# Three graph layers and an edge-gated layer on one core: the end of a layer woven into its last turns

## The reference

```python
for i in range(3):
    msg = h[src]
    agg = segment_sum(msg, dst);  cnt = segment_sum(ones, dst)
    h = (agg / clip(cnt, 1)[:, None]) @ Wl[i] + bl[i] + h @ Wr[i]
    if i < 2: h = relu(h)
x = layernorm(x + h)
```

## Time and profile before

| what | value |
|---|---|
| three runs, us | 3498.85, 3500.41, 3501.01 (median 3500.41) |
| profiled execution, us | 3502.18, span 3500.4 |
| busy share of the span | PE 76%, POOL 67%, DVE 61%, ACT 35% |
| gathers of the three layers on POOL | 1584, 1538.5 us busy |
| mean granted TensorE clock | 0.905 of full speed |

### The profile page before, as it was taken

One profiled execution on the slowest core, in us unless ns is written; L12 is line 12 of the kernel. 1 busy time (PEld: TensorE's weight loads), 2 busy tenths in 40 slices (PEclk: granted clock), 3 DMA queues, 4 the chain that ended last, 5 costly groups with the idle time before them and its releaser, 6 DMA issues.

```text
span 3500.4 us, 71571 instructions
## 1 busy us (share of the span) xinstructions
PE 2665.2 (76%) x16221; PEld 2000.1 (57%) x16222; DVE 2142.4 (61%) x4932; ACT 1216.7 (35%) x1668; POOL 2333.4 (67%) x2399
## 2 busy tenths in 40 slices
PE   6578988656787775567887855678888888888884
PEld 5345555556564555555555555556666666666653
DVE  6644554446532234467454454668888888888886
ACT  2422333002000000020000000368888888888865
POOL 3567777575777777746777777357777777767610
PEclk8799999777899997788999977899999999999987
DMA  4354444223565562236887642254444444444411
GB/s 149 104 180 147 145 129 145 76 50 108 160 168 146 139 161 60 53 104 205 250 240 222 192 122 58 78 154 126 128 126 127 127 126 127 124 114 121 114 52 37
DMA packets 345986, 454.45 MB, mean 130 GB/s; under 512 B 135643, under 2 KB 260599, under 8 KB 342311
## 3 DMA queue, kind: packets, MB, share of 16 engines
q0 software_dynamic: 88624, 207.58, 21.9%
q10 hardware_dynamic: 101984, 181.27, 16.2%
q1 hardware_dynamic: 155304, 64.77, 7.1%
HBM read 357.03 MB, written 101.90 MB: 131 GB/s over the span
## 4 chain that ended last, share of the span: by engine, by line
POOL 35%; PE 21%; issue 19%; DVE 10%; DMA 9%; DVEq 3%; SPq 2%; ACT 2%; POOLq 0%; ACTq 0%
POOL shared L760 28%; POOL shared L800 8%; DMA shared<-q_dram,idx 6%; PE ps L955 6%; PE ps L946 4%; PE ps L1151 3%; PE ps L938 2%; SPq L638 1%; DVE work L2326 1%; PE ps L965 1%; DVE work L2010 1%; PE ps L1154 1%; DMA counts_dram<-work 1%; DVE work L2335 1%; ACT work L1481 1%
## 5 line engine op out<-in xcount | busy, mean ns | idle before, releaser
L760 POOL DMA_INDIRECT shared<-y_dram,idx x1584 | 1538.5, 971 | 623.3 <-issue 498.9
L946 PE MATMUL ps<-shared,work 128*128 x4368 | 683.0, 306 | 389.9 <-SPq L578 190.6
L800 POOL DMA_INDIRECT shared<-q_dram,idx x784 | 777.6, 992 | 284.0 <-issue 204.9
L946 PEld LDWEIGHTS ps<-shared,work 128*128 128x128 f32 x4368 | 618.6, 216 | 466.7 <-issue 457.1
L2037 DVE TENSOR_TENSOR acc<-acc,ps 128x129 f32 x546 | 156.3, 286 | 901.8 <-PE ps L946 770.9
L1151 PE MATMUL ps<-pq,work 128*128 x1664 | 498.8, 402 | 149.9 <-issue 89.6
L2326 DVE TENSOR_TENSOR work<-ps,shared 128x256 f32<-128x256 f32 x832 | 294.6, 416 | 177.6 <-PE ps L1154 149.4
L1151 PEld LDWEIGHTS ps<-pq,work 128*128 128x128 f32 x1664 | 257.5, 195 | 244.3 <-issue 173.6
L965 PE MATMUL ps<-pq,work 128*128 128x385 bf16 x1456 | 294.1, 352 | 73.2 <-DVE pq L2007 31.3
L1452 ACT ACTIVATE pq<-ps,blT_sb 128x512 f32<-128x512 f32 (+1 forms) x28 | 16.5, 631 | 887.6 <-PE ps L1050 887.6
L1333 ACT CAST work<-ps 128x600 bf16<-128x600 f32 x260 | 159.6, 661 | 339.6 <-PE ps L938 312.5
(11 more groups left out here) (363 smaller groups left out, 3627.2 us busy)
## 6 DMA issues: line engine op xcount, KB each, us to landing
work<-counts_dram ACTq DMA_DIRECT2D x156, 384.0 KB
counts_dram<-work ACTq DMA_DIRECT2D x26, 1568.0 KB
shared<-y_dram,idx POOLq DMA_INDIRECT x1584
ea_parts<-work ACTq DMA_DIRECT2D x128, 196.0 KB
ea_sb<-ea_parts SPq DMA_DIRECT2D x196, 128.0 KB
work<-counts_dram ACTq DMA_DIRECT2D x52, 416.0 KB
shared<-q_dram,idx POOLq DMA_INDIRECT x784
y_dram<-work SPq DMA_DIRECT2D x21, 448.0 KB, 3.0
```

What stands on the lines that cost most here:

```text
L760: pool.indirect_dma_start(msg[:, u, 0:F], None, y_dram, bass.IndirectOffsetOnAxis(ap=idx[:, u:u + 1], axis=0)).then_inc(s_quad[q], 16)
L800: pool.indirect_dma_start(q_ring[:, u * 2 * F:(u + 1) * 2 * F], None, q_dram, bass.IndirectOffsetOnAxis(ap=idx[:, u:u + 1], axis=0)).then_ ...
L946: last = te.matmul(ps[:, SUM_BANKS[i], 0:FA], lhsT=oh4[:, OH_SLOTS[i], u, :], rhs=shared[:, bass.ds(place + u * FA, FA)], start=u == 0, st ...
```

## The change

The end of layers 1 and 2 is moved into the last turns of pairs. `dst` is sorted, so low windows are complete before high ones: from turn `TAIL` = 3 on, turn 3 + c works on chunk c, for c from 0 to 5. Chunk 6 is done after the last turn. Within such a turn DVE computes the new rows after item 0 and clears that seventh of `acc` after item 1, PE transposes after item 2, multiplies with Wl after item 4 and with Wr after item 6, all through one place in PSUM (`ps_tail`, banks 6 and 7); ACT does the relu, all copies and the store of y. Since gathers still read this layer's y then, the next layer's y goes to another home in DRAM: `y_two[0]` for layers 1 and 3, `y_two[1]` for layer 2. New rows and staged y lie in `shared`, over parts of the split that are used up.

In layers 1 and 2 the one-hots of the pair turns take `iota`, as `ps_tail` shares bank 7 with `iota_ps`. `conv_rows` moves into layer 1, after POOL's first 48 gathers, with a wait on `y_split`; the copy to `dst_sorted` moves ahead of the first index loads on SP; the columns are made in the first pair turn of layer 1. The loops over pair turns of these layers are written out.

```diff
-        y_dram = dram("y_dram", (NP, F))
+        y_two = [dram("y_even", (NP, F)), dram("y_odd", (NP, F))]
...
+        h_two = [shared[:, Y_AT + k * CW * F:Y_AT + (k + 1) * CW * F].rearrange("p (u f) -> p u f", f=F) for k in range(2)]
+        y_next = [shared[:, Y_AT + k * CW * F:Y_AT + (k + 1) * CW * F].rearrange("p (u f) -> p u f", f=F) for k in range(2, 4)]
...
+        ps_tail = ps_flat[:, 6 * 512:6 * 512 + CW * F].rearrange("p (u f) -> p u f", f=F)
...
+        TAIL = DTURNS - NCH + 1
...
@@ sync
+            with sp.If(unsorted < 1):
+                sp.dma_start(dst_sorted, dst[0:EP].rearrange("(t e) -> t e", e=P)).then_inc(s["idx_given"], 16)
             sp.wait_ge(s["chosen"], 9)
...
                 first_indices()
-                for it in range(NCH):
-                    sp.wait_ge(s["prod_act"], ((layer + 1) * NCH + it + 1) * 2 + 1)
-                    sp.wait_ge(s["prod_dve"], ((layer + 1) * NCH + it + 1) * 2 + 1)
-                    sp.dma_start(y_dram[it * CW * P:(it + 1) * CW * P, :].rearrange("(u p) f -> p u f", p=P),
-                                 y_staged(it % 2)).then_inc(s[Y_SENT[it % 2]], 16)
...
@@ gpsimd
             def conv_rows():
                 pool.wait_ge(s["idx_given"], 16)
                 pool.wait_ge(s["tki"], 1)
+                pool.wait_ge(s["y_split"], NCH)
...
-                            msg[:, u, 0:F], None, y_dram,
+                            msg[:, u, 0:F], None, y_two[layer % 2],
...
                     for q in range(FIRST_SLOTS, RQ):
                         gathers(0, q)
+                    conv_rows()
...
             sage_gathers(0)
-            conv_rows()
@@ tensor
-                with pe.Fori(0, DTURNS) as b:
+                def both(b, after=None):
                     places = load_turn(b + WOVEN)
                     pairs = load_pairs(b)
                     for i in range(IT):
                         item(b + WOVEN, i, places[i])
                         pair_item(b, i, pairs[i])
+                        if after is not None:
+                            after(i)
...
+                def chunk_after(it):
+                    def after(i):
+                        if i == 2:
+                            transposes(layer, it)
+                        if i == 4:
+                            y_products(layer, it, ps_tail)
+                        if i == 6:
+                            res_products(layer, it, ps_tail)
+                    return after
...
+                    for b in range(TAIL):
+                        both(b, columns_after if layer == 0 and b == 0 else None)
+                    for b in range(TAIL, DTURNS):
+                        both(b, chunk_after(b - TAIL))
+                    transposes(layer, NCH - 1)
+                    y_products(layer, NCH - 1, ps_first(0))
+                    res_products(layer, NCH - 1, ps_first(1))
...
+            def transposes(layer, it):
+                c = layer * NCH + it
+                pe.wait_ge(s["dlo_ready"], 1)
+                if c:
+                    pe.wait_ge(s["res_kept"], c * 2)
+                for k, wins in enumerate(QUADS):
+                    pe.wait_ge(s["h_ready"], c * CW + wins[-1] + 1)
+                    for u in wins:
+                        last = te.transpose(ps_tail[:, u, :], h_two[it % 2][:, u, :], ident[:, :])
+                    last.then_inc(s["h_transposed"], 1)
...
@@ scalar
-                relu(0)
                 for it in range(NCH):
                     c = layer * NCH + it
+                    y_ps, res_ps = (ps_tail, ps_tail) if it < NCH - 1 else (ps_first(0), ps_first(1))
                     for k, wins in enumerate(QUADS):
                         act.wait_ge(s["h_transposed"], c * 2 + k + 1 + 1)
-                        sc.activation(h_all[...], ps_tr[...], ACT.Relu, ...)
+                        sc.activation(h_all[...], ps_tail[...], ACT.Relu, ...)
+                    if it >= 2:
+                        act.wait_ge(s[Y_SENT[it % 2]], y_sent(layer, it - 2))
+                    for k, wins in enumerate(QUADS):
+                        act.wait_ge(s["products"], c * 2 + k + 1)
+                        sc.copy(y_next[it % 2][:, wins[0]:wins[-1] + 1, :], y_ps[:, wins[0]:wins[-1] + 1, :]).then_inc(s["prod_act"], 1)
+                    act.wait_ge(s["prod_act"], (NCH + c) * 2 + 3)
+                    alone(act)
+                    act.dma_start(y_two[(layer + 1) % 2][it * CW * P:(it + 1) * CW * P, :].rearrange("(u p) f -> p u f", p=P),
+                                  y_next[it % 2]).then_inc(s[Y_SENT[it % 2]], 16)
+                    for k, wins in enumerate(QUADS):
+                        act.wait_ge(s["res_ready"], c * 2 + k + 1)
+                        sc.copy(chunk(res, it, F)[...], res_ps[...]).then_inc(s["res_kept"], 1)
@@ vector
-                onehots(layer, it * IT + (i + OHS - 1), columns[i], OH_SLOTS[(i + OHS - 1) % IT])
+                onehots(layer and not beside_tail, it * IT + (i + OHS - 1), columns[i], OH_SLOTS[(i + OHS - 1) % IT])
...
-                       in0=(iota_ps if layer else iota[:, :])           # pair_onehots
+                       in0=(iota_ps if layer == 2 else iota[:, :])
...
                         add_pair(layer, b, i, p_sums, p_columns)
+                        if conv and i == 5:
+                            conv_columns_known()
+                        if ending is not None and i == 0:
+                            dve.wait_ge(s["counts_put"], pair_added(layer, b, i))
+                            new_h(layer, ending)
+                        if ending is not None and i == 1:
+                            clear(layer, ending)
...
+                    for b in range(TAIL, DTURNS):
+                        both(b, ending=b - TAIL)
+                    dve.wait_ge(s["added_items"], (layer + 1) * NI1 + OHS)
+                    dve.wait_ge(s["counts_put"], pairs_added(layer + 1))
+                    new_h(layer, NCH - 1)
+                    clear(layer, NCH - 1)
...
+            def new_h(layer, it):
+                c = layer * NCH + it
+                if not layer:
+                    inverse_counts(it)
+                if c >= 2:
+                    dve.wait_ge(s["h_transposed"], c * 2 - 1)
+                for u in range(CW):
+                    w = it * CW + u
+                    v.scalar_tensor_tensor(
+                        out=h_two[it % 2][:, u, :], in0=acc[:, w * FA:w * FA + F], scalar=inv[:, w:w + 1],
+                        in1=res[:, w * F:(w + 1) * F], op0=ALU.mult, op1=ALU.add).then_inc(s["h_ready"], 1)
+
+            def clear(layer, it):
+                dve.wait_ge(s["h_ready"], layer * NW + (it + 1) * CW)
+                v.memset(acc[:, it * (CW * FA):(it + 1) * (CW * FA)], 0.0).then_inc(s["acc_clear"], 1)
...
-                v.memset(acc[:, :], 0.0).then_inc(s["acc_clear"], NCH)
```

More of the change, by code:

```diff
@@ L915, in sage_sums @@
                 pe.wait_ge(s["prod_act"], (layer + 1) * (NCH * 2) + 1)
[L916 removed]
+                pe.wait_ge(s["prod_dve"], NCH * 2 + 1)
                 if layer:
@@ new lines, in sage_sums @@
+                if layer == 2:
+                    pe.wait_ge(s["dlo_ready"], 1)
+                    with pe.Fori(0, DTURNS) as b:
+                        both(b)
+                else:
+                    for b in range(TAIL):
[5 more added lines that the diff above has]
+                    res_products(layer, NCH - 1, ps_first(1))
@@ new lines, in y_products, with res_products @@
+            def y_products(layer, it, to):
+                c = layer * NCH + it
+                for k, wins in enumerate(QUADS):
+                    pe.wait_ge(s["h_copied"], c * 2 + k + 1 + 1)
+                    for u in wins:
+                        last = te.matmul(to[:, u, :], lhsT=h_all[:, it * CW + u, :], rhs=w0_sb[:, layer + 1, 0:F], start=True, stop=True)
+                    last.then_inc(s["products"], 1)
+            def res_products(layer, it, to):
+                c = layer * NCH + it
+                for k, wins in enumerate(QUADS):
+                    if it < NCH - 1:
+                        pe.wait_ge(s["prod_act"], (NCH + c) * 2 + k + 1 + 1)
+                    for u in wins:
+                        last = te.matmul(to[:, u, :], lhsT=h_all[:, it * CW + u, :], rhs=w0_sb[:, layer + 1, F:2 * F], start=True, stop=True)
+                    last.then_inc(s["res_ready"], 1)
@@ L1085, in _ @@
+            for layer in range(3):
+                sage_sums(layer)
             pe.wait_ge(s["added_items"], 3 * NI1 + OHS)
@@ L1453, in relu @@
                                       ACT.Relu, bias=blT_sb[:, layer:layer + 1]).then_inc(s["h_copied"], 1)
-                relu(0)
-                for it in range(NCH):
-                    c = layer * NCH + it
-                    if it + 1 < NCH:
-                        relu(it + 1)
-                    act.wait_ge(s["y_free"], c + NCH)
-                    act.wait_ge(s["products"], c * 2 + 1)
```

(24 more changed lines are left out.)

132 lines of the change are left out of this document (35 added, 97 removed).

## The result

The changed kernel takes 3456.18 us (median of four, 3452.32 to 3456.57), the kernel before 3499.63 on the same chip: ratio 0.9872, interval 0.9860 to 0.9884. The profiled execution took 3456.49 with a span of 3454.7, so the two traces differ by 45.7.

What follows compares the result with a forecast made beforehand. POOL's gathers and its stops were taken as the bound; -31.1 (layer ends) - 13.5 (layer starts) + 11 (one-hots) + 8.8 (new rows) = -24.8, from the median 3500.4 to 3475 us, range 3465 to 3492.

Steps and rivals of the forecast that it cites:

- What bounds: Layers 1 to 3: a layer lasts as long as its 528 gathers, changing only if gathers lengthen or POOL stands still.
- End of layers: Ends of layers 1 and 2: only the seventh chunk is left, so first gathers come 15.0 and 16.1 us earlier.
- (e): Layer ends: seventh chunk lacks an empty pipe because chunk 5 is late; gain under 28 us; included in likeliest case's 0.50.
- Start of layers 2 and 3: Index-load stops some 65 us into each layer shrink because the split of y begins earlier: 13.5 us gained.
- One-hots of layer 2: Layer 2's pair turns: one-hots reading iota from SBUF instead of PSUM hold POOL's gathers, costing 11 us.
- Rival (b): Layer 2's one-hots cost what layer 1's dense stretch shows, 21.8 us instead of 11: 3486; chance 0.14.
- (d): POOL is held through most two-input DVE work beside gathers: at 90%, 90 us against 44.6 gained, 3546; chance 0.07.
- New rows beside the gathers: Six chunks in each of layers 1 and 2: seven-instruction DVE runs of 1.92 us hold gathers, costing 8.8 us.
- Rival (a): New rows cost POOL almost nothing, as it is released after each instruction: 3.5 us or under, 3470; chance 0.18.
- In layer 1 nothing changes here: Layer 1's pair turns already take one-hots from iota, so their cost to gathers stays the same: no term.
- Small things: Moved row conversion, dst copy, extra DVE and PE work and stores on ACT's queue: hidden or idle, priced at nothing.
- (c): PE becomes the bound in the tail turns, losing 2 us more in each of 12: 3499, no change; chance 0.11.

Runs made afterwards that it cites:

- the late read: Changed kernel, with ACT waiting for the first landed quad of layers 2 and 3 before reading y back for the split: 3467.38 us, ratio 0.9902.
- Runs of 14 and 21: Changed kernel, new-rows instructions of a chunk done twice (14 unbroken): 3484.81 us; three times (21): 3510.04 us, or 3491.61 with the real rows first.
- early rows: Kernel before, with POOL's seven row gathers after its first 48 gathers and the dst copy ahead of the first index loads: 3498.74 us, ratio 0.9999.
- a pause: One 0.4 us DVE clearing ahead of layer 1's pair turns: 3500.03 us in the kernel before, 3457.59 us in the changed kernel.
- two homes: Kernel before, with y in two homes in DRAM and nothing else: 3498.85 us against 3500.69, ratio 0.9994.
- three runs of seven: Changed kernel, new rows done three times, with DVE waiting for its own seventh and fourteenth instruction: 3476.16 us, ratio 0.9928.

## Why the prediction was right or wrong

**What bounds** was right: a layer is as long as its gathers and POOL's stops. **End of layers** (-15.0, -16.1): -15.8 and -15.1, together 30.9 against 31.1. The residual products of chunk 5 were out of the way in time, as assumed; (e) did not occur. **Start of layers 2 and 3** (-13.5): -6.2 and -5.4, 11.6; the late read shows that the mechanism is the one given. **One-hots of layer 2** (+11): 10.0 in the trace (6.8 by wide ones, 3.2 by narrow), 7.9 to 9.3 in the medians of the runs that put them in and took them out. The size was taken from layer 1's held gathers, which the change itself made fewer, so that so close a hit is in part luck. Rival (b) fell, (d) as well.

**The step that failed is "New rows beside the gathers"**: +8.8, measured about +1.4. I priced a run of 1.92 us by a share of its time, 38%, taken from a run of 8.10 us. The price isn't a share of the run. The gathers of 1.7 us there had each waited some 0.77 for one subtraction of 1.0 us to pass; a new-rows instruction is followed by the next after 0.26, and a gather waited 0.14 at most for one. Runs of 14 and 21 cost 1.5 and 3.1 a chunk, as they held a gather to their end. The 6.41 us gather isn't explained by any of this: it began 0.49 us into six subtractions and was held to their end. Rival (a) is what happened, and 1.4 in place of 8.8 makes the forecast 3468, which is still inside the range. The rule of the Trainium skill that stood behind this step (SBUF — State Buffer, Who interferes with whom), a lock for one instruction, agrees with the runs of seven (1.08), not with the gather of 3.90 that saw eleven instructions go by.

**"In layer 1 nothing changes here"** failed too, and that took the time out of the range. Its pair turns have the same one-hots, yet these held its last 130 gathers for 7.0 us instead of 12.3 (7.7 with the new rows), and layer 1 as a whole came out 7.9 shorter, not 4.4 longer. With rows and one-hots of layer 1 as measured my sum is -30.9 - 11.6 + 10.0 + 1.4 - 5.3 = -36.4. The 9 us that remain to the 45.7 between the traces are 5.3 behind layer 3 (scatter, as the other runs show), some 3 in layer 1 outside these holds, and 1 in layer 3; to the 43.4 between the medians 7 remain. Why layer 1's turns were held less is not settled: written-out turns and early rows each show part of it in one trace, a pause moves nothing. The prediction gave the written-out turns no term at all; alone they took some 5 us off the median of the kernel before.

**Small things** that were priced at nothing were nothing in the medians (rows early, two homes). **(c)** did not occur, POOL sets the pace in the changed kernel; but with 4 us more DVE work in a turn (the three runs of seven) most likely DVE, not PE, ended layer 1 nine us late. The signs named were these: gap 19 (18.4), stops gone (one of 2.97 stayed), mean 1.00 to 1.01 in layer 2 (1.00), PE below 85% (75% at most); layer 1's 4 us more was the false one.

## What to carry to other kernels

Price an overlap by the length of one instruction and of the unbroken run, not by a share taken from other runs: here seven two-input DVE instructions in a row cost the gathers beside them 0.1 us, 14 cost 1.5 and 21 cost 3.1, and a wait after every seventh brought 21 back to 0.1 (by the break or by the shift in time, which was not separated). Work that is moved beside a bound engine is better not fed from where that engine reads: giving the one-hots their PSUM operand back was worth 16.6 us, more than a third of what the whole move had won. Where a gain is larger than the sum of its steps, compare also the parts that "did not change".

## What the runs showed of the hardware that was not expected

A gather that began some 2 us or more into an unbroken run of DVE instructions with two SBUF inputs was held to its very end (2.58 us beside 14, 3.90 beside 21), but for one at 2.06 us, while one that began up to 1.2 us into the same run lost 0.14 at most, but for one chunk of 14. All 36 gathers held so began 0.15 to 0.18 us after the beginning of one of the DVE instructions, which come every 0.262 us; the one at 2.06 us began 0.22 after. Pauses that made the 21 instructions only 0.27 us longer ended the holds, and moved these moments as well. Why a gather is let in early in a run and not later was not tried.

TensorE's mean granted clock in layer 1's pair turns was 0.93 of full speed (2.4 GHz) in both stretches, where it had been 0.81 and 0.78; PE was busy 55.30 of 74 us and 66.77 of 94, before 53.48 of 73 and 59.10 of 101. In layer 2 it stayed near the old level (0.78 and 0.85). The runs don't show whether this shortened layer 1.
